# Residual add of a cross-attention kernel: a ring of tiles in SBUF against a copy in HBM with accumulating DMAs

## The reference

```python
q = (tgt @ Wq.T).reshape(B, N, NH, dk).transpose(0, 2, 1, 3)
k = (memory @ Wk.T).reshape(B, N, NH, dk).transpose(0, 2, 1, 3)
v = (memory @ Wv.T).reshape(B, N, NH, dk).transpose(0, 2, 1, 3)
scores = jnp.einsum('bhqd,bhkd->bhqk', q, k) * scale
probs = jax.nn.softmax(scores, axis=-1)
att = jnp.einsum('bhqk,bhkd->bhqd', probs, v)
att = att.transpose(0, 2, 1, 3).reshape(B, N, D)
tgt2 = att[0]
return tgt + tgt2
```

## Time and profile before

| what | value |
|---|---|
| time, median of 3 executions (lowest to highest) | 229.81 us (229.1 to 230.04) |
| span of the profiled execution, first to last instruction | 225.9 us |
| busy: TensorE / VectorE / ScalarE / GpSimd | 157.9 / 156.8 / 111.6 / 88.4 us |
| HBM read / written | 37.75 / 33.55 MB |
| mean DMA rate over the span | 316 GB/s |

### The profile page before, as it was taken

The page is one execution under the profiler, slowest core; times in us unless marked ns, Lnnn a source line. Parts: engine busy times, 40 slices in busy tenths (PEclk is TensorE's granted clock), DMA queues, the critical chain, the costliest instruction groups (busy, mean ns, idle before and its releaser), DMA issues.

```text
span 225.9 us, 3447 instructions
## 1 busy us (share of the span) xinstructions
PE 157.9 (70%) x1213; PEld 121.1 (54%) x1213; DVE 156.8 (69%) x235; ACT 111.6 (49%) x285; POOL 88.4 (39%) x50
## 2 busy tenths in 40 slices
PE   7899999998868596889339774992978299610000
PEld 7788888886647465656216553661665178400000
DVE  0716365256897889978994899799889985289300
ACT  2544446019839474797218553890857198500000
POOL 4000000000466496606940694079339700079600
PEclk9999999999996979999956995898599769985555
DMA  6999999999999999999999999999999999929998
GB/s 220 352 389 389 385 389 386 386 385 388 387 211 170 195 141 201 123 152 181 160 359 395 387 389 289 316 317 254 389 401 391 400 407 405 404 109 379 373 383 319
DMA packets 53373, 71.47 MB, mean 316 GB/s; under 512 B 1648, under 2 KB 27248, under 8 KB 53360
## 3 DMA queue, kind: packets, MB, share of 16 engines
q1 hardware_dynamic: 53360, 71.31, 104.0%
HBM read 37.75 MB, written 33.55 MB: 316 GB/s over the span
## 4 chain that ended last, share of the span: by engine, by line
issue 31%; DMA 24%; POOL 23%; SPq 13%; POOLq 2%
POOL ring L280 23%; DMA ring<-in_x_dram 14%; DMA out_dram<-ring 10%; SPq L212 7%; SPq L204 3%; POOLq L56 2%; SPq L231 1%; SPq L226 1%; SPq L223 0%; SPq L224 0%; SPq L221 0%; POOLq L280 0%; POOLq L285 0%; POOLq L277 0%; SPq L216 0%
## 5 line engine op out<-in xcount | busy, mean ns | idle before, releaser
L280 POOL TENSOR_TENSOR ring<-ring,att 128x512 f32<-128x512 f32 (+2 forms) x43 | 86.0, 2031 | 123.4 <-DVE att L507 115.9
L342 PE MATMUL bank<-k_t,q_diag 128*128 128x512 f32 x192 | 68.6, 473 | 18.9 <-DVE q_diag L478 18.9
L438 ACT ACTIVATE probs<-bank,neg_max 128x512 f32<-128x512 f32 x64 | 44.6, 698 | 42.5 <-DVE neg_max L484 42.1
L478 DVE TENSOR_TENSOR q_diag<-q_t,q_diag 32x128 fp32r<-32x128 f32 x64 | 53.2, 831 | 1.1 <-ACT q_diag L427 0.4
L484 DVE TENSOR_REDUCE neg_max<-bank 128x1 f32<-128x512 f32 x64 | 43.5, 685 | 14.5 <-PE bank L342 14.1
L374 PE MATMUL bank<-ident,probs 128*128 128x128 f32 x256 | 44.8, 303 | 7.6 <-ACT probs L438 7.5
L342 PEld LDWEIGHTS bank<-k_t,q_diag 128*128 128x128 f32 x192 | 37.2, 223 | 23.5 <-DVE q_diag L478 19.9
L432 ACT COPY probs_t<-bank 128x512 f32<-128x512 f32 x64 | 37.6, 587 | 21.2 <-PE bank L374 21.0
L374 PEld LDWEIGHTS bank<-ident,probs 128*128 128x128 f32 x256 | 31.7, 153 | 25.1 <-ACT probs L438 19.6
L523 DVE TENSOR_TENSOR ring<-ring,bank 128x512 f32<-128x512 f32 (+2 forms) x20 | 23.9, 1210 | 0.1
L427 ACT CAST q_diag<-q_t 32x128 fp32r (+1 forms) x64 | 18.9, 295 | 0.6
(11 more groups left out here) (35 smaller groups left out, 86.0 us busy)
## 6 DMA issues: line engine op xcount, KB each, us to landing
ring<-in_x_dram SPq DMA_DIRECT2D x28, 1024.0 KB, 13.1
out_dram<-ring SPq DMA_DIRECT2D x14, 1024.0 KB, 12.8
out_dram<-ring SPq DMA_DIRECT2D x28, 256.0 KB, 10.1
out_dram<-ring SPq DMA_DIRECT2D x14, 512.0 KB, 11.2
x_first<-in_x_dram SPq DMA_DIRECT2D x4, 768.0 KB, 13.9
out_dram<-x_first SPq DMA_DIRECT2D x2, 1024.0 KB, 9.2
wq_raw<-in_L_xattn_Wq_dram SPq DMA_DIRECT2D x2, 512.0 KB, 5.4
x_first<-in_x_dram SPq DMA_DIRECT2D x2, 512.0 KB, 5.4
```

Source lines behind the costliest of these rows:

```text
L280: nc.gpsimd.tensor_tensor(xs, xs, a.unsqueeze(1).to_broadcast([P, BPG, a.shape[1]]), ALU.add).then_inc((tail_added if tail else added)[g], 1)
L342: last = mm(bank[:, h % S_BANKS, :], q_diag[:, a, h % Q_SLOTS, :], k_t[:, g, b, :], start=((a, b) == PASSES[0]), stop=((a, b) == PASSES[-1]))
L438: nc.scalar.activation(probs[:, h % 2, :], bank[:, h % S_BANKS, :], ACT.Exp, bias=neg_max[:, h:h + 1], scale=1.0, accum_out=row_sum[:, h:h ...
L478: last = nc.vector.tensor_tensor(q_diag[rows, LO, slot, :], q_t[rows, g, bass.ds(j * P, P)], q_diag[rows, HI, slot, :].bitcast(F32), ALU.s ...
```

## The change

x is no longer brought to SBUF, but for x[0]. The sync engine issues 32 plain DMAs after the inputs of the attention, one for each batch, that copy x to the output within HBM; each moves 1.05 MB as 16 runs of 64 KB. They are counted in eight semaphores `copied[s]`, four batches each. GpSimd no longer adds. It waits for `att_ready` of tile j, then for each group s for `copied[s]`, and issues an accumulating DMA that reads tile j of `att` from SBUF four times and adds it to the four batches' rows in the output: 32 such DMAs, 1.05 MB of output each, in rows of 2 KB. VectorE's adds, the second multiplication of `normalize` and the parts of a tile are gone; each tile is turned back and normalized once, into its own quarter of a larger `att`. The ring, its waits and the overlaid slots are gone, and the tiles of the projections have room of their own. The kernel ends when all 32 accumulating DMAs have landed. The attention's arithmetic is the same.

```diff
-    TAIL_POOL_GROUPS = (1, 3, 6)
+    COPIES = 8
+    BPC = B // COPIES
...
-    x_rows = x.rearrange("b (j p) d -> p j b d", p=P)
+    x0_rows = x[0].rearrange("(j p) d -> p j d", p=P)
+    x_whole = x.rearrange("(s b) (u n) d -> s b u (n d)", s=COPIES, u=16)
+    out_whole = out.rearrange("(s b) (u n) d -> s b u (n d)", s=COPIES, u=16)
     out_rows = out.rearrange("b (j p) d -> p j b d", p=P)
...
-        x_first = sb("x_first", [P, T, BPG, D])
...
+        x0_raw = sb("x0_raw", [P, T, D])
+        ctx_raw = sb("ctx_raw", [P, T, D])
+        wq_raw = sb("wq_raw", [P, C, D])
+        wk_raw = sb("wk_raw", [P, C, D])
+        wv_raw = sb("wv_raw", [P, C, D])
+        x0_t = sb("x0_t", [P, C, 2, N], F32R)
+        wk_t = sb("wk_t", [P, C, 2, D], F32R)
+        w_t = sb("w_t", [P, C, 2, D], F32R)
+        ctx_t = sb("ctx_t", [P, C, 2, N], F32R)
...
-        att = sb("att", [P, D])
+        att = sb("att", [P, T, D])
...
-        loaded = [None] + [sem(f"loaded{g}") for g in range(1, G)]
-        added = [sem(f"added{g}") for g in range(G)]
-        tail_added = [sem(f"tail_added{g}") for g in range(G)]
-        stored = [sem(f"stored{g}") for g in range(G)]
+        copied = [sem(f"copied{s}") for s in range(COPIES)]
+        accumulated = sem("accumulated")
...
-            def store(j, g, part=None):
-                if j == T - 1:
-                    sp.wait_ge(tail_added[g], 1)
-                else:
-                    sp.wait_ge(added[g], unit(j, part) + 1)
-                cols = unit_cols(j, part) if j in IN_PARTS else slice(0, D)
-                sp.dma_start(out_rows[:, j, g * BPG:(g + 1) * BPG, cols], x_slot(j, g, cols)).then_inc(stored[g], 16)
-
-            def reload(j, g):
-                sp.wait_ge(stored[g], (unit(j) + 1) * 16)
-                sp.wait_ge(loaded[g], (j + 2) * 16)
-                load(j + 2, g)
...
-            sp.dma_start(x_first[:, 0, 1:BPG, :], x_rows[:, 0, 1:BPG, :]).then_inc(first_loaded, 16)
-            for g in range(1, CTX_RAW + 1):
-                load(0, g)
...
+            for s in range(COPIES):
+                for b in range(BPC):
+                    sp.dma_start(out_whole[s, b, :, :], x_whole[s, b, :, :]).then_inc(copied[s], 16)
+            sp.wait_ge(accumulated, T * COPIES * 16)
...
-            def add_unit(j, part=None):
-                cols = unit_cols(j, part)
-                pool.wait_ge(att_ready, unit(j, part) + 1)
-                tail = isinstance(j, int) and j == T - 1
-                for g in TAIL_POOL_GROUPS if tail else POOL_GROUPS:
-                    pool.wait_ge(loaded[g], (j + 1) * 16)
-                    xs = x_slot(j, g, cols)
-                    a = att[:, cols]
-                    nc.gpsimd.tensor_tensor(xs, xs, a.unsqueeze(1).to_broadcast([P, BPG, a.shape[1]]),
-                                            ALU.add).then_inc((tail_added if tail else added)[g], 1)
-
-            for part in range(parts(0)):
-                add_unit(0, part)
-            with pool.Fori(1, T - 1) as j:
-                for part in range(parts(j)):
-                    add_unit(j, part)
-            add_unit(T - 1)
+            for j in range(T):
+                pool.wait_ge(att_ready, j + 1)
+                for s in range(COPIES):
+                    pool.wait_ge(copied[s], BPC * 16)
+                    pool.dma_start(out_rows[:, j, s * BPC:(s + 1) * BPC, :],
+                                   att[:, j, :].unsqueeze(1).to_broadcast([P, BPC, D]),
+                                   accum_op=ALU.add).then_inc(accumulated, 16)
...
-            def turn_back(j, part=None):
-                groups = unit_groups(j, part)
-                pe.wait_ge(att_t_ready, j * HG + groups.stop)
-                if not (isinstance(j, int) and unit(j, part) == 0):
-                    pe.wait_ge(added[DVE_GROUPS[-1]], unit(j, part))
-                for g in groups:
+            def turn_back(j):
+                pe.wait_ge(att_t_ready, (j + 1) * HG)
+                if not (isinstance(j, int) and j == 0):
+                    pe.wait_ge(att_ready, j)
+                for g in range(HG):
                     last = nc.tensor.transpose(att_ps[:, g * P:(g + 1) * P], att_t[:, g, :], ident[:, :])
                 last.then_inc(att_back, 1)
...
-            def normalize(j, part=None):
-
-                cols = unit_cols(j, part)
-                hs = slice(cols.start // DK, cols.stop // DK)
-                dve.wait_ge(att_back, unit(j, part) + 1)
-                dve.wait_ge(recip_ready, j * HG + hs.stop // HPG)
-                if j > 0:
-                    before = [p for p in range(parts(j - 1)) if unit_cols(j - 1, p).start < cols.stop][-1]
-                    dve.wait_ge(added[POOL_GROUPS[-1]], unit(j - 1, before) + 1)
-                back = att_ps[:, cols].rearrange("p (h d) -> p h d", d=DK)
-                inverse = recip[:, hs].unsqueeze(2).to_broadcast([P, hs.stop - hs.start, DK])
-                nc.vector.tensor_tensor(att[:, cols].rearrange("p (h d) -> p h d", d=DK), back, inverse,
+            def normalize(j):
+                dve.wait_ge(att_back, j + 1)
+                dve.wait_ge(recip_ready, (j + 1) * HG)
+                back = att_ps.rearrange("p (h d) -> p h d", d=DK)
+                inverse = recip[:, :].unsqueeze(2).to_broadcast([P, HEADS, DK])
+                nc.vector.tensor_tensor(att[:, j, :].rearrange("p (h d) -> p h d", d=DK), back, inverse,
                                         ALU.mult).then_inc(att_ready, 1)
-                nc.vector.tensor_tensor(back, back, inverse, ALU.mult).then_inc(att_ps_ready, 1)
-
-            def add(j, g, part=None):
-                cols = unit_cols(j, part)
-                dve.wait_ge(att_ps_ready, unit(j, part) + 1)
-                if g == 0:
-                    if isinstance(j, int) and j == 0:
-                        dve.wait_ge(first_loaded, 16)
-                    else:
-                        dve.wait_ge(first_rest_loaded, (T - 1) * 16)
-                else:
-                    dve.wait_ge(loaded[g], (j + 1) * 16)
-                xs = x_slot(j, g, cols)
-                a = att_ps[:, cols]
-                nc.vector.tensor_tensor(xs, xs, a.unsqueeze(1).to_broadcast([P, BPG, a.shape[1]]),
-                                        ALU.add).then_inc((tail_added if j == T - 1 else added)[g], 1)
-
-            def heads(j, more, adds):
-
-                adds = list(adds)
+
+            def heads(j, more):
                 for h in range(MAX_AHEAD, HEADS):
-                    if adds and (j <= 1 or (h - MAX_AHEAD) % 2 == 0):
-                        add(*adds.pop(0))
                     head_max(j, h)
                     if h % HPG == 2 and h > HPG:
                         invert_sums(j, h // HPG - 1)
...
                     if h - AHEAD in laid_out_at(more):
                         g = (h - AHEAD + Q_SLOTS) // HPG
                         query_low(j + g // HG, g % HG)
-                    done = (h + 1 - AHEAD) // HPG - 1
-                    if (h + 1 - AHEAD) % HPG == BACK and part_ending(j, done) is not None:
-                        normalize(j, part_ending(j, done))
-                        adds = [(j, g, part_ending(j, done)) for g in DVE_GROUPS]
-                while adds:
-                    add(*adds.pop(0))
...
-            heads(0, True, [])
-            normalize(0)
-            for j in range(1, T):
-                heads(j, j + 1 < T, [(j - 1, g) for g in DVE_GROUPS])
+            for j in range(T):
+                heads(j, j + 1 < T)
                 normalize(j)
-            for g in TAIL_DVE_GROUPS:
-                add(T - 1, g)
```

More of the change, by code:

```diff
@@ L157, in as_dest @@
             return ps.rearrange("p (c n) -> p c n", n=P) if len(dest.shape) == 3 else ps
[L160 to L176, removed]
-            cols = unit_cols(j, part)
[L179 to L188, removed]
-            if g == 0:
-                return x_first[:, j, :, cols]
-            return ring[:, (j % 2) * RING + (g - 1), :, cols]
         def laid_out_at(more):
@@ L226, in _ @@
                 sp.dma_start(to[:, :, :], rows.rearrange("(t p) d -> p t d", p=P)).then_inc(loads, 16)
-            held_until = {CTX_RAW: last_job["ctx_t"], WV_RAW: last_job["wv_t"], X0_T: last_job["queries"],
-                          X0_T + 1: last_job["queries"], WK_T: last_job["keys"], WK_T + 1: last_job["keys"]}
-            half_used, all_used = (W_T, CTX_T), (W_T + 1, CTX_T + 1)
-            sp.dma_start(x_first[:, 0, 1:BPG, :], x_rows[:, 0, 1:BPG, :]).then_inc(first_loaded, 16)
-            for g in range(1, CTX_RAW + 1):
-                load(0, g)
-            for j in range(1, T):
-                sp.dma_start(x_first[:, j, 1:BPG, :], x_rows[:, j, 1:BPG, :]).then_inc(first_rest_loaded, 16)
-            for g in range(CTX_RAW + 1, G):
-                sp.wait_ge(bank_filled, held_until[g - 1])
-                load(0, g)
-            for slot in (X0_T + 1, WK_T, WK_T + 1) + half_used + all_used:
```

(23 more changed lines are left out.)

31 lines of the change are left out of this document (3 added, 28 removed).

## The result

293.89 us (median of 4, 293.15 to 294.97) against 229.45 us before (228.44 to 230.04): ratio 1.284, 95% interval 1.278 to 1.290. The kernel is slower by 64 us. The time was forecast at 350.2 us with a range of 260 to 440.

The account below looks back on a forecast made before the run. DMA traffic was taken as the bound, with the attention close behind. Inputs 16.5, copies 164.9 and accumulations 164.9 made 346.3 us; with 3.9 us around the span, 350.2 us, range 260 to 440.

Parts of the forecast that it names:

- inputs: Start of the DMA work: the attention's 5.24 MB of inputs come first and end at 16.5 us.
- copy, 33.55 MB: Copies of x within HBM: 67.1 MB of reads and writes share a 407 GB/s ceiling, 164.9 us.
- accumulation, 33.55 MB: Accumulating DMAs into the output: 164.9 us, the middle value between 82.4 and 223.7 us.
- signs of being wrong: In the profile after: copies finished before 110 us, end below 300 us, idle DMA engines last, accumulation well below 200 GB/s.
- its 200: Stretch from 20 to 80 us, as a sign of being right: some 200 GB/s counted once.
- the rival's 400: Same stretch from 20 to 80 us if both ceilings are the engines': 400 GB/s; that rival had 26%.
- two reasons: For the accumulation's 164.9 us: either both reads by the DMA engines count, or both directions of HBM.
- the rival of the engines' ceilings: DMA work: engines set both ceilings, copy 82.4 us, accumulation with two reads 164.9, total 267.7 us; chance 26%.
- Slow rows: Accumulations: each 2 KB row is read, added and written slowly; 409 us, 458 or 326 in variants; chance 20%.
- Faster: DMA work: only delivered bytes count, 185 us, then the attention decides, about 195 to 200 us; chance 7%.
- Issue on GpSimd: Issuing each accumulating DMA: between 0.51 and 4.5 us, hidden; would count only from 8.2 us each.
- the floor of 50 + 110 = 160 us: Attention's end: TensorE alone is busy 110 us after 50, so the last tile can't be normalized before 160; 165 expected.

Follow-up runs that it names:

- experiment 1: The changed kernel with its copies and attention but without any accumulating DMA (the output is x): 164.74 us.
- Experiment 5: The changed kernel with at most 12 accumulations under way, each waiting by a semaphore for the one twelve before it: 283.76 us, ratio 1.245.
- experiment 6: The changed kernel with the accumulations going to a four-slot tile in SBUF instead of the output, copies kept: 297.9 us (one run).
- experiment 3: The changed kernel with accumulations in rows of 4 KB instead of 2 KB, two tiles at a time, still 32 DMAs: 282.53 us, ratio 1.237.
- experiment 2: The changed kernel with the same 32 DMAs from GpSimd as plain stores of att, without the add: 210.04 us, ratio 0.920.
- experiments 9 and 10: The kernel before with tile 0 stored in halves instead of quarters (234.94 us, ratio 1.028), and with every tile whole (243.89 us, ratio 1.067).
- 11: The kernel before with groups 6 and 7 copied and accumulated by DMA, GpSimd adding three pieces a tile instead of five: 241.01 us, ratio 1.054.
- experiment 7: The changed kernel with copies as 32 DMAs in rows of 2 KB instead of runs of 64 KB: 301.97 us (one run).
- experiment 10: The kernel before with every tile whole and rows of 2 KB in all stores: 243.89 us, ratio 1.067.

## Why the prediction was right or wrong

**That the kernel becomes slower, and bound by DMA: right.** The end is a run of accumulations, 128 us beyond the last tile, with TensorE, VectorE and ScalarE idle.

**The sum.** The forecast was 56.3 us too high:

| term | forecast | measured | difference |
|---|---|---|---|
| inputs | 16.5 | 16.5 (not measured apart) | 0 |
| copy, 33.55 MB | 164.9 | 100.8 (333 GB/s, experiment 1) | -64.1 |
| accumulation, 33.55 MB | 164.9 | 162.1 (207 GB/s) | -2.8 |
| DMA engines run dry | 0 | 11.5 (what is left of the span) | +11.5 |
| around the span | 3.9 | 3.0 | -0.9 |

The dips worked out by themselves are 7 x (1 - 81 / 207) + 22 x (1 - 124 / 207) = 13 us, 1.5 more than the remainder; some of it lies at the very end, where the last DMAs run out. Experiment 5, which removes the dips, gained 10 us. The measured time lies within the forecast range, but one of its own signs of being wrong came true: "an end below 300 us". From 17 to 75 us 340 GB/s moved, neither its 200 nor the rival's 400.

**The step that failed** is the copy's: "the rate is the same whether the traffic is all reads (387) or reads and writes mixed (401), which looks like one shared ceiling". Every transfer of the trace before has one end in HBM, so these rows could not carry that, as the prediction itself had said. A copy loads HBM twice and runs at 333. The Trainium skill's figure for copies (DMA: Bandwidth & Descriptors, "Latency and other measured facts": 214 GB/s in each direction, there for tiles of 128 x 16 KiB) does not hold for these copies, 333 in runs of 64 KB and 317 in rows of 2 KB; the measurement decides.

**The accumulation's term was right, with one of its two reasons.** HBM's two directions don't set it: the copies had 667 GB/s of HBM traffic (experiment 1), and without HBM the rate is no higher (experiment 6). The reason left is the engines' second read; the numbers fit it (414 GB/s of reads), and no run parts it from the adding itself. That the reason that failed for the copy gave the right number here is luck in part.

**The rivals.** What happened is nearest to the rival of the engines' ceilings (267.7 us): add 18.4 us because a copy runs at 333 and not at 407, and 11.5 us of dips, and take off the 3.7 us of the two small differences. Its chance of 26% against 42% was too low. Slow rows: refuted by experiment 3 (212 GB/s in rows of 4 KB). Faster: refuted by experiment 2, which is 18.5 us faster than before just because it leaves the add out; an add at no cost did not exist.

**Issue on GpSimd.** 1.28 us each, within the 0.51 to 4.5 us given. That GpSimd could stop after 15 DMAs was not thought of; it cost 10 us (experiment 5).

**The engines: right, the last tile partly by luck.** VectorE fell by 68 us (69 forecast), the low halves to 0.28 us, and the last tile was normalized at 162 us (165 forecast). But the floor of 50 + 110 = 160 us was none: the 110 us were TensorE's at a granted clock of 0.87, and the same work took 95.7 us at 1.00. TensorE was idle for the other 16 of the 112 us, which the forecast did not count.

**What bounded the kernel before: half right.** The DMA engines were full, but for tile 0 with slow packets that filled a wait: experiments 9 and 10 gave the rows back their rate and lost time, 11 gave the attention back its pace at the price of DMA work and lost time too. That the kernel before stands where both limits meet is the reading that fits all of them; no run relieves one limit alone. The prediction's reading of the rows left two things out: the last slice has a DMA share of 8 tenths as well, and the largest share of the chain that ended last is "issue" with 31%, time in which an engine waited for nothing that the profile shows.

Left open: why a copy within HBM runs at 333 and not at 387. The length of its rows and its queue are not the reason; whether it is HBM at 667 GB/s or the engines' own side to it was not tried. Open too is whether the second read or the adding halves an accumulation.

## What to carry to other kernels

An add in a DMA is not free: price each kind of transfer by its own rate, here 387 to 400 GB/s for a load or a store, 333 for a copy within HBM, 207 for an accumulation. Copy and accumulation take 7.8 us per MB together, load and store 5.1, so in a kernel whose DMA engines are full it doesn't pay to give them the adds, however much it relieves VectorE. DMA engines that are full in every slice are no proof that they set the time; look whether slow packets fill a wait for something else. Where GpSimd issues many DMAs, let it wait by a semaphore before it stops by itself (here at 12 under way, where it stopped after 15).

## What was not expected of the hardware

GpSimd, once it has stopped after 15 accumulating DMAs, goes on only when the DMA engines have nearly run out of its work: 62 us of standing and then 7 us at 81 GB/s instead of 207. Copies in packets of 64 KB hold their rate against accumulations in rows of 2 KB (322 GB/s in all from 80 to 118 us, with five accumulations waiting), while copies in rows of 2 KB share with them and both together fall to 262 GB/s (experiment 7). And the 32-partition operations of VectorE take 0.29 us at most beside GpSimd's DMA issues, but up to 2.38 us beside GpSimd's adds, and up to 4.5 us in experiment 10, where these adds have 2048 columns.
